# Sums by head: products of messages and weights on VectorE instead of GpSimd, weight columns on ScalarE

## The reference

```
a = jnp.exp(a - amax[edge_dst])
a = a / (jax.ops.segment_sum(a, edge_dst, num_segments=n)[edge_dst] + 1e-12)
ns = jax.ops.segment_sum(vs * a[..., None], edge_dst, num_segments=n)      # 8 heads x 8 scalars
nv = jax.ops.segment_sum(vv * a[..., None, None], edge_dst, num_segments=n) # 8 heads x 4 vectors x 3
```

## Time and profile before

| what | value |
|---|---|
| median of 3 runs | 12285.94 us (12283.43 to 12288.8) |
| the profiled execution, its own time | 12286.25 us |
| its span from first to last instruction | 12284.4 us |
| the stage of the sums, first `rel` to the end of the last addition | 5486.41 to 6517.20 us |
| iterations in it | 130 |
| busy in the whole span | PE 8811.9, DVE 8307.3, POOL 6391.2, ACT 5973.8 us |

### The profile page before, as it was taken

The page is one execution under the profiler, slowest core; times in us unless marked ns, Lnnn a source line. Parts: engine busy times, 40 slices in busy tenths (PEclk is TensorE's granted clock), DMA queues, the critical chain, the costliest instruction groups (busy, mean ns, idle before and its releaser), DMA issues. The chain is left out here.

```text
span 12284.4 us, 201080 instructions
## 1 busy us (share of the span) xinstructions
PE 8811.9 (72%) x51550; PEld 7117.1 (58%) x51550; DVE 8307.3 (68%) x20853; ACT 5973.8 (49%) x14810; POOL 6391.2 (52%) x5659
## 2 busy tenths in 40 slices
PE   2478888888888888817774444458888888888866
PEld 1256666666666666617773333346666666666656
DVE  3268888777777777767784333347777777777754
ACT  0167777776777777700000000026666666666642
POOL 0077777777777777718871000015555555555520
PEclk7589999999999999958885555569999999999988
DMA  1133333333333333325551000014444444444443
GB/s 34 49 95 106 104 106 104 105 104 104 104 104 104 105 103 106 103 90 174 173 176 41 18 18 12 18 56 144 146 146 143 146 144 146 145 145 144 147 121 107
DMA packets 1025152, 1301.80 MB, mean 106 GB/s; under 512 B 356442, under 2 KB 662016, under 8 KB 1024516
## 3 DMA queue, kind: packets, MB, share of 16 engines
q1 hardware_dynamic: 773636, 838.93, 21.1%
q0 software_dynamic: 251136, 459.61, 14.6%
HBM read 830.83 MB, written 467.10 MB: 106 GB/s over the span
## 5 line engine op out<-in xcount | busy, mean ns | idle before, releaser
L1460 POOL DMA_INDIRECT conv_src<-conv_table,conv_pair x1872 | 1933.6, 1033 | 1711.5 <-DVE conv_prod L1623 1125.0
L1551 ACT ACTIVATE conv_scaled<-conv_onehot,conv_pair 128x128 f32<-128x128 f32 x5592 | 1659.2, 387 | 1251.2 <-DVE conv_onehot L1589 1211.8
L573 POOL DMA_INDIRECT att_dstg<-dst_table,att_rec x1680 | 1804.5, 1074 | 511.9 <-issue 508.6
L573 POOL DMA_INDIRECT att_srcg<-src_table,att_rec x1680 | 1780.8, 1060 | 528.5 <-issue 499.4
L632 PE MATMUL att_banks<-att_ident,att_ch 128*128 128x128 f32 (+1 forms) x5004 | 724.4, 282 | 768.1 <-ACT att_chT L721 768.1
L632 PEld LDWEIGHTS att_banks<-att_ident,att_ch 128*128 128x128 f32 (+1 forms) x5004 | 559.2, 139 | 978.5 <-ACT att_chT L721 867.2
L1493 PE MATMUL conv_banks<-conv_w_last,conv_hid 64*128 64x224 f32 x1858 | 625.2, 418 | 627.2 <-DVE conv_prod L1623 626.5
L1506 PE MATMUL conv_banks<-conv_prod,conv_onehot 128*128 128x192 f32 x3712 | 1070.3, 372 | 0.0
L1086 PE MATMUL attend_banks<-attend_wm,attend_onehot 128*128 128x168 f32 x4160 | 752.2, 350 | 385.7 <-POOL attend_wm L1067 164.7
L645 PE MATMUL att_banks<-att_w_b,att_chT 128*128 128x224 f32 x3328 | 1020.8, 389 | 0.0
L1633 DVE SCALAR_TENSOR_TENSOR conv_acc<-conv_acc,conv_keep,conv_banks 128x320 f32<-128x320 f32 x1856 | 898.0, 508 | 121.7 <-PE conv_banks L1515 120.2
(11 more groups left out here) (339 smaller groups left out, 22924.5 us busy)
## 6 DMA issues: line engine op xcount, KB each, us to landing
agg<-conv_acc SPq DMA_DIRECT2D x928, 288.0 KB, 2.9
attend_msg<-messages SPq DMA_DIRECT2D x520, 320.0 KB, 3.0
messages<-att_msg SPq DMA_DIRECT2D x416, 320.0 KB
conv_pair<-in_conv_rec SPq DMA_DIRECT2D x944, 70.0 KB
att_es<-in_att_es SPq DMA_DIRECT2D x212, 256.0 KB, 3.1
conv_src<-conv_table,conv_pair POOLq DMA_INDIRECT x1872
out_row<-agg SPq DMA_DIRECT2D x14, 2016.0 KB, 10.1
att_srcg<-src_table,att_rec POOLq DMA_INDIRECT x1680
```

The costliest lines, as they stand in the source:

```text
L573: g.indirect_dma_start(out=rows[slot][:, u, :], out_offset=None, in_=table[:, :], in_offset=bass.IndirectOffsetOnAxis(ap=rec[q][:, UNIT * ...
L1460: g.indirect_dma_start(out=src[q][:, u, 0, :], out_offset=None, in_=x_table[:, :], in_offset=bass.IndirectOffsetOnAxis(ap=ends[q][:, u // ...
L1551: last = s.activation(scaled[h][:, u, d, :], onehot[h][:, u, :], ACT.Copy, scale=geo[q][:, u // 2, u % 2, PLANE_AT[d]:PLANE_AT[d] + 1])
```

## The change

The two product instructions move from POOL to DVE, behind the one-hot compare of the same iteration, and raise `wm_done` there. The copy of the weight columns moves from POOL to ACT, with a semaphore of its own, `keys_done`, for which PE waits as well. ACT loads its table at the start of the phase. SP's release for the transfers of j waits for `wm_done` and `keys_done` instead of `wm_done` and `rel_done`. POOL keeps only the `iota` at the start.

```diff
@@ SP
-                        hold(sp, sp_passed, (wm_done, j - 1), (rel_done, j - 1))
+                        hold(sp, sp_passed, (wm_done, j - 1), (keys_done, j - 1))
@@ POOL -> ACT
-                def weigh(j, h, i):
-                    pool.wait_ge(landed[h], LAND * (i + 1))
+            @block.scalar
+            def _(act):
+                s = nc.scalar
+                s.preload_act_table_set(TABLES)
+
+                def keys(j, h, i):
+                    act.wait_ge(landed[h], LAND * (i + 1))
                     if not isinstance(j, int):
-                        pool.wait_ge(agg_done, G * (j - 1))
-                    p_ = kd[h][:, :, 0:HEADS]
-                    for lo, hi in ((0, S), (S, FEAT)):
-                        n = (hi - lo) // HEADS
-                        g.tensor_tensor(wm[h][:, :, lo:hi].rearrange("p u (n c) -> p u n c", n=HEADS),
-                                        msg[h][:, :, lo:hi].rearrange("p u (n c) -> p u n c", n=HEADS),
-                                        bc(p_, 3, n), ALU.mult)
-                    g.tensor_copy(wm[h][:, :, FEAT:MSG], p_).then_inc(wm_done, 1)
+                        act.wait_ge(agg_done, G * (j - 1))
+                    s.activation(wm[h][:, :, FEAT:MSG], kd[h][:, :, 0:HEADS], ACT.Copy).then_inc(keys_done, 1)
@@ PE, aggregate
                     pe.wait_ge(wm_done, j + 1)
+                    pe.wait_ge(keys_done, j + 1)
@@ DVE, one_hots, behind the compare
+                    for lo, hi in ((0, S), (S, FEAT)):
+                        last = v.tensor_tensor(wm[h][:, :, lo:hi].rearrange("p u (n c) -> p u n c", n=HEADS),
+                                               msg[h][:, :, lo:hi].rearrange("p u (n c) -> p u n c", n=HEADS),
+                                               bc(kd[h][:, :, 0:HEADS], 3, (hi - lo) // HEADS), ALU.mult)
+                    last.then_inc(wm_done, 1)
```

More of the change, by code:

```diff
@@ L1020, in phase_attend @@
         wm = [a.sb(f"wm{h}", [P, T, MSG]) for h in range(2)]
-        (tables, numbered, rel_done, oh_done, wm_done, agg_done, acc_done, sp_passed) = (a.sem(n) for n in (
-            "tables", "numbered", "rel_done", "oh_done", "wm_done", "agg_done", "acc_done", "sp_passed"))
+        (tables, numbered, keys_done, rel_done, oh_done, wm_done, agg_done, acc_done, sp_passed) = (a.sem(n) for n in (
+            "tables", "numbered", "keys_done", "rel_done", "oh_done", "wm_done", "agg_done", "acc_done", "sp_passed"))
         landed = [a.sem(f"landed{h}") for h in range(2)]
@@ L1055, in _ @@
                        allow_small_or_imprecise_dtypes=True).then_inc(numbered, 1)
-                def weigh(j, h, i):
-                    pool.wait_ge(landed[h], LAND * (i + 1))
-                    if not isinstance(j, int):
-                        pool.wait_ge(agg_done, G * (j - 1))
-                    p_ = kd[h][:, :, 0:HEADS]
-                    for lo, hi in ((0, S), (S, FEAT)):
-                        n = (hi - lo) // HEADS
-                        g.tensor_tensor(wm[h][:, :, lo:hi].rearrange("p u (n c) -> p u n c", n=HEADS),
-                                        msg[h][:, :, lo:hi].rearrange("p u (n c) -> p u n c", n=HEADS),
-                                        bc(p_, 3, n), ALU.mult)
-                    g.tensor_copy(wm[h][:, :, FEAT:MSG], p_).then_inc(wm_done, 1)
-                weigh(0, 0, 0)
-                weigh(1, 1, 0)
-                with pool.Fori(1, QUAD_ITERS // 2) as i:
+            @block.scalar
[4 more added lines that the diff above has]
+                    act.wait_ge(landed[h], LAND * (i + 1))
+                    if not isinstance(j, int):
+                        act.wait_ge(agg_done, G * (j - 1))
+                    s.activation(wm[h][:, :, FEAT:MSG], kd[h][:, :, 0:HEADS], ACT.Copy).then_inc(keys_done, 1)
+                keys(0, 0, 0)
+                keys(1, 1, 0)
+                with act.Fori(1, QUAD_ITERS // 2) as i:
                     for h in range(2):
-                        weigh(2 * i + h, h, i)
+                        keys(2 * i + h, h, i)
             @block.tensor
```

## The result

The kernel after takes 12130.01 us (median of 4 runs, 12118.45 to 12136.57), the kernel before 12286.12 us on the same chip (12283.43 to 12288.8): a ratio of 0.9872, 95% interval 0.9858 to 0.9887. It is faster, as forecast, but by 156 us where 72 were forecast, and the time lies 64 us under the lower end of the range.

What follows compares the result with a forecast made beforehand. The stage was taken as bound by weighing plus reloading a buffer, with DVE the next bound at 7.345 us an iteration. Stage 958.6 us against 1030.8, so 12286.25 - 72 = 12214 us; range 12194 to 12259.

Steps and rivals of the forecast that it cites:

- reading of the bound: Stage of the sums: POOL and DVE take turns reading; weighing plus reloading a buffer takes 15.88 us per two iterations.
- the sum of 7.02 us: Stage of the sums: one buffer's weighing on POOL, from the products' start to the copy's end, read from one turn.
- The products: Two products moved to DVE: 1.14 and 1.67 us, 2.81 together, where POOL alone needs 4.75.
- The pattern rival: DVE's products slowed by weight columns 9 apart: 1.88 ns an element, 280 us over forecast, 12494 us; chance 0.05.
- DVE's iteration: DVE in the stage: key, compare, products (5.26 us) plus four additions (2.085) make 7.345 us, the new bound.
- The register reads: DVE's four block numbers for its additions, read behind the products: hidden, counted as nothing; uncovered up to 2.24 us.
- The strict emptying of the pipe: DVE's next instruction waits for the pipe to empty: 0.22 us an iteration, 29 us, 12243 us; chance 0.04.
- The release: `wm_done` for SP's transfers comes 5.34 us after landing instead of 7.02; buffer loop 14.2 us per two iterations.
- the first rival: Loads set the stage's pace: a load 1.0 us longer gives 7.6 us an iteration, 12246 us; chance 0.12.
- The copy on ACT: Weight columns copied on ACT while the compare runs: nearest row 387 ns, covered, cost nothing.
- PE: PE's group of 32 takes 6.5 us, under 7.3, so not waited for; rival as bound 12442 us, chance 0.03.
- The sum: Whole stage: start, 128 iterations x 7.345, end and a late load make 958.6 us against 1030.8, 72 less.

Runs made afterwards that it cites:

- e3: Kernel before with only the copy of the weight columns moved from GpSimd to ScalarE, products staying on GpSimd; ratio 0.9968 on a late chip, stage 931.0 us.
- e5: Kernel after with DVE's products put ahead of `rel` and the compare, so buffers are free earlier; 12108.66 us, ratio 0.9865.
- e12: Kernel before with eight inert memsets added once to DVE's program ahead of the stage's zeros; 12211.26 us against 12280.69, ratio 0.9942.
- e14: Kernel before with a table load and eleven small copies added to ACT's program, DVE's and GpSimd's as before; 12279.27 us against 12280.69, ratio 0.9995.
- e16: Kernel before with only the weight columns' copy moved from GpSimd to ScalarE, on a late chip; 14040.07 us against 14031.78, ratio 1.0016.
- e1: Kernel before with eight inert memsets added once to DVE's program ahead of the stage's zeros, on a late chip; 14418.38 us, ratio 0.9993.

## Why the prediction was wrong, by its own steps

**Its reading of the bound** was right: two engines taking turns, and a loop of weighing and reloading. `e3` confirms the loop with another weighing, 7.02 worked out and 6.98 measured. What I missed there is that the order of the turns was worth 120 us of the stage, without any product being moved. The turn that I read was one of several kinds: in 39 of 130 the copy stands behind a compare, which the sum of 7.02 us leaves out.

**The products** cost what was forecast. The next instruction starts 6001.30 - 5998.50 = 2.80 us behind their start, forecast 2.81; as single instructions 1219 and 1751 ns, forecast 1.2 and 1.75. The pattern rival is dead: 1.04 ns an element, not 1.26.

**DVE's iteration**: 7.31 us, forecast 7.345. From compare to products it is 2.21 in place of 2.24; the additions to the next `rel` take 1.93 and 2.25. The register reads are hidden: the addition at 6001.30 has no idle time ahead of it. The strict emptying of the pipe would have made it 7.57.

**The release**: the buffer of the `rel` at 5996.08 is free at 6001.38, 5.30 us later (forecast 5.34), and its next load is there at 6010.01, 0.69 us before DVE asks at 6010.70. DVE waits for transfers 2.9 us in the whole stage, where over 20 would have spoken for the first rival, and `e5` shows it from the other side.

**The copy on ACT** takes 0.31 us (estimate 0.39) and nobody waits for it. **PE** is waited for 6.2 us in all.

**The sum is the step that failed.** Its stage was right, 958.6 us forecast and 956.6 measured, with two small errors against each other (128 periods of 7.31 in place of 7.345 are 4.5 us less, the start and the end some 2 more). But it took the 72 us from the time of before and left every other phase as it was, a term put at nothing without a reason. The runs put in its place: the change makes DVE's program longer by 8 instructions in all (two in each of four written-out `one_hots`), which moves the convolution's loop, and its edge costs 2.0 us less in each of 28 passes. That is shown: 8 inert instructions alone do it (`e12`, convolution 58 us shorter, kernel 69), and a kernel in which DVE's program is unchanged does not have it (`e14`, 0.9995). The account of the 167.8 us of span is: stage 74.2, convolution 67.7 (of them 55 at the edges, the rest unplaced), ahead of the stage 25.2, 0.7 elsewhere. 74 of the stage and 69 of `e12` make 143 of the 156 us between the medians; the other 13 are not placed.

**Left open.** Why the attention phase, which lies *ahead* of the changed code, is 9 to 25 us shorter on chips like the first in every kernel with a longer DVE program and not in `e14` (its gathers 4598.5 to 4609.1 us against 4618.1 and 4623.0, one traced execution each); it lies in a loop of its own with a branch, I found no edge there of one length, and only 12 packets of instructions arrive in the whole phase, so it is not the same thing once more. Whose instructions the packets at the edge bring, and why their number falls from 3 to 1 with the place. Why the gathers are 12 ns shorter, and why on the late chips the attention phase gets longer in the same kernels. And the product move without the copy's, of which there is no measurement.

## What to carry to other kernels

Work out a stage from its own rows, and then ask of every edit what it does to the *rest of the program*: instructions added to an engine move all its later loops, and here this was worth nearly as much as the edit itself (69 and 74 us). If a written-out loop stands still once a pass, count the packets of instructions there in the DMA view. Before a small gain is put down to an idea, run a control that only moves the code: a few inert instructions on the same engine. And where two engines take turns, look first at the order of the turns: let the short user of the loop that bounds go first (copy off GpSimd, the small product on GpSimd, the large one at the head of DVE's work), before work is taken off one of them altogether; the split gave a ratio of 0.9771 where the full move gave 0.9872, both on chips like the first. And measure on another chip too: of the over 120 us that the stage of `e16` gained, nothing reached the total.

## What the runs showed of the hardware

- DVE stands still once in each pass of a written-out loop for 4.4, 2.8, 2.5, 1.8 or 1.6 us, depending on whether its program has 0, 4, 8, 16 or 32 more instructions ahead of it, and 3, 2, 2, 2 or 1 packets of instructions arrive just then. At the loop's start, with no branch back, it is 1.87 or 1.48 us.
- A GpSimd product of two fp32 inputs alone takes 1.97 us for 1024 elements in each partition and 2.83 for 1536, some 1.9 ns an element; DVE takes 1.22 and 1.75.
- The same program, the kernel before with 8 inert instructions, takes 12211.26 us on one chip (`e12`) and 14418.38 on another (`e1`). Of the 2227 us between their traced spans 1703 lie in the gathers of the attention phase and 504 in the convolution, the two phases whose gathers GpSimd issues.
